# A pre-norm transformer layer on one core: the feed-forward part spread over two batches' steps, GpSimd's order and the PSUM banks changed

## What is computed

```python
x = x + attn(layernorm(x), W_qkv, W_out)      # 32 query heads, 16 key/value heads of 64, causal, ALiBi
P = einsum('bsd,dr->bsr', layernorm(x), U1)   # 256 -> 64
H = gelu(einsum('bsr,rf->bsf', P, V1) + b1)   # 64 -> 1024
Q = einsum('bsf,fr->bsr', H, U2)              # 1024 -> 64
x = x + einsum('bsr,rd->bsd', Q, V2) + b2     # 64 -> 256
```

## Time and profile before

| | us |
|---|---|
| device time, median of 3 runs | 2876.21 (2874.03 to 2881.04) |
| the profiled execution's own time | 2881.05 |
| its span, first to last instruction | 2879.3 |
| PE busy | 2680.9 (93%) |
| ACT busy | 2184.7 (76%) |
| POOL busy | 2011.7 (70%) |
| DVE busy | 1992.4 (69%) |

### The profile page before, as it was taken

The page is one execution under the profiler, slowest core; times in us unless marked ns, Lnnn a source line. Parts: engine busy times, 40 slices in busy tenths (PEclk is TensorE's granted clock), DMA queues, the critical chain, the costliest instruction groups (busy, mean ns, idle before and its releaser), DMA issues.

```text
span 2879.3 us, 83610 instructions
## 1 busy us (share of the span) xinstructions
PE 2680.9 (93%) x31112; PEld 1834.4 (64%) x31112; DVE 1992.4 (69%) x6731; ACT 2184.7 (76%) x3892; POOL 2011.7 (70%) x1816
## 2 busy tenths in 40 slices
PE   4999999999999999999999999999999999999986
PEld 1566666766666666666766667666666766667663
DVE  6767676776766767676776776767677676767753
ACT  3777878778787777878778787777878778787782
POOL 1667777777777767777677777777777677777783
PEclk8999999999999999999999999999999999999996
DMA  6444443444434344343544434344343444435420
GB/s 170 96 100 88 94 90 79 104 91 91 89 87 99 82 97 88 87 97 78 105 90 93 89 84 101 85 94 87 88 99 81 98 91 91 92 77 105 87 61 20
DMA packets 495146, 260.82 MB, mean 91 GB/s; under 512 B 317962, under 2 KB 493066, under 8 KB 494474
## 3 DMA queue, kind: packets, MB, share of 16 engines
q1 hardware_dynamic: 494740, 255.47, 40.8%
...
## 4 chain that ended last, share of the span: by engine, by line
PE 71%; ACT 8%; DVE 7%; issue 7%; POOL 5%; DMA 1%; SPq 0%; DVEq 0%; ACTq 0%; POOLq 0%
PE proj L450 31%; PE scores L450 17%; PE o_acc L450 13%; PE max_scores L450 4%; PE ffn_acc L450 4%; ACT h_f L830 2%; POOL p_lo L1090 2%; DVE max_scores L930 2%; ACT p_hi L700 2%; POOL o_hi_lo L1098 2%; ACT p_f L741 2%; ACT L741 1%; DVE h_hi L1022 1%; DMA o_t<-in_L_attn_W_out 1%; POOL h_lo L1118 1%
## 5 line engine op out<-in xcount | busy, mean ns | idle before, releaser
L1090 POOL TENSOR_TENSOR p_lo<-p_f,p_hi 128x512 f16<-128x512 f32 x1280 | 1474.4, 1159 | 564.6 <-ACT p_hi L700 564.4
L741 ACT ACTIVATE p_f<-scores 128x512 f32<-128x512 f32 x1280 | 755.6, 590 | 130.0 <-PE scores L450 126.2
L700 ACT ACTIVATE p_hi<-p_f 128x512 f16<-128x512 f32 x1280 | 800.4, 625 | 14.8
L930 DVE CUSTOM_DVE_ANT_0 max_scores<-max_scores,causal 128x384 f32<-128x384 f32 (+3 forms) x1184 | 563.3, 507 | 268.7 <-PE max_scores L450 257.7
L450 PE MATMUL scores<-q_hi_lo,k_lo_hi 128*128 128x512 f16 (+3 forms) x2048 | 614.2, 300 | 0.2 <-ACT p_f L741 0.2
L450 PE MATMUL scores<-q_hi_aug,k_hi_aug 128*128 128x512 f16 (+3 forms) x2048 | 586.5, 299 | 0.0
L450 PE MATMUL o_acc<-v_hi_one,p_lo 128*128 128x65 f16 x5120 | 518.9, 195 | 42.9 <-POOL p_lo L1090 39.9
L450 PEld LDWEIGHTS o_acc<-v_hi_one,p_lo 128*128 128x128 f16 x5120 | 471.1, 98 | 90.7 <-POOL p_lo L1090 63.2
L450 PE MATMUL o_acc<-v_hi_one,p_hi 128*128 128x65 f16 x5120 | 518.3, 194 | 0.0
L450 PE MATMUL o_acc<-v_lo,p_hi 128*128 128x64 f16 x5120 | 517.9, 193 | 0.0
L450 PEld LDWEIGHTS o_acc<-v_lo,p_hi 128*128 128x128 f16 x5120 | 468.7, 99 | 37.8
...
## 6 DMA issues: line engine op xcount, KB each, us to landing
q_hi_aug<-q_pair_hi SPq DMA_DIRECT2D x512, 64.0 KB, 2.0
q_hi_lo<-q_pair_hi SPq DMA_DIRECT2D x512, 64.0 KB, 2.0
q_hi_lo<-q_pair_lo SPq DMA_DIRECT2D x512, 64.0 KB, 2.0
k_hi_aug<-k_pair_hi SPq DMA_DIRECT2D x256, 64.0 KB, 2.0
k_lo_hi<-k_pair_hi SPq DMA_DIRECT2D x256, 64.0 KB, 2.0
k_lo_hi<-k_pair_lo SPq DMA_DIRECT2D x256, 64.0 KB, 2.0
...
```

The lines of the kernel that those rows point to most:

```text
L700: return nc.scalar.activation(out_ap, in_ap, ACT.Copy, scale=scale)
L741: nc.scalar.activation(p_f[:, k % 3, :], score_bank[k % 2][:, :], ACT.Exp).then_inc(exp_done, 1)
L930: last = nc.vector.tensor_tensor_reduce(out=bank, in0=bank, in1=causal[:, (T - 1 - qt) * P:S], scale=1.0, scalar=-3e38, op0=ALU.add, op1=A ...
L1090: nc.gpsimd.tensor_tensor(p_lo[:, slot, n, :], p_f[:, k % 3, :], p_hi[:, slot, n, :], ALU.subtract).then_inc(lo_p, 1)
```

## The change

**The feed-forward part is spread.** `FFN_PAIRS` becomes `H_PAIRS` at (13, 1), (15, 1) and, in the next body, (1, 1) and (3, 1), placed ahead of the row maxima in TensorE's segment; the casts and GpSimd's subtractions go one segment later (`SPLIT_PAIRS`); the second products go to (14, 3), (0, 3), (2, 3), (4, 3), the last step to (5, 0) and (5, 3) and the store to the end of step 5. A short body in mode TAIL, steps 0 to 5, is added at the end for the last batch.

**The second products are summed in SBUF.** Each pair has a `proj` bank of its own, and VectorE copies the first into `q_sum` and adds the other three. `ffn_acc` is gone as such; the row maxima have two banks throughout.

**GpSimd's order.** The fifth `p_lo` comes before `o_lo` in segment 0. The power for the first layer norm moves from the end of step 7 to (8, 2), the four of the second from (8 + t, 4) to (9 + t, 0). **VectorE's order and the banks**: transposing the row maxima moves from segment 1 to 2, the second layer norm one segment later.

```diff
-MAX_SEG, K_SEG, V_SEG, O_SEG = 1, 0, 4, 4
+MAX_SEG, K_SEG, V_SEG, O_SEG = 2, 0, 4, 4
-VE1_AT, NMR1_AT = (7, 4), (8, 2)
+VE1_AT, RS1_AT, NMR1_AT = (7, 4), (8, 2), (8, 4)
-RSTD2_AT = {(8 + t, 4): t for t in range(T)}
-LN2_AT = {(9 + t, 1): t for t in range(T)}
-LN2_T_AT = {(9 + t, 2): t for t in range(T)}
+RSTD2_AT = {(9 + t, 0): t for t in range(T)}
+LN2_AT = {(9 + t, 2): t for t in range(T)}
+LN2_T_AT = {(9 + t, 3): t for t in range(T)}
-FFN_PAIRS = {(13, 1): 0, (13, 3): 1, (14, 0): 2, (14, 2): 3}
-U2_PAIRS = {(13, 4): 0, (14, 0): 1, (14, 2): 2, (14, 4): 3}
-QF_AT, Y_AT = (15, 1), (15, 4)
+H_PAIRS = {(13, 1): 0, (15, 1): 1, (1, 1): 2, (3, 1): 3}
+SPLIT_PAIRS = {(13, 2): 0, (15, 2): 1, (1, 2): 2, (3, 2): 3}
+U2_PAIRS = {(14, 3): 0, (0, 3): 1, (2, 3): 2, (4, 3): 3}
+QF_AT, Y_AT, STORE_AT = (5, 0), (5, 3), 5
 def q_lag(s):
-    return 0 if s >= 13 else 1
+    return 1
         def max_place(s, n):
-            k, total = SEG * s + n, SEG * KV
-            back = next(j for j in range(1, total) if in_ffn_bank((k - j) % total) == in_ffn_bank(k))
-            return (ffn_bank if in_ffn_bank(k) else max_bank), back
+            return max_bank[(SEG * s + n) % 2], 2
             body(Count(B), LAST)
+            body(Count(B + 1), TAIL)
+        def ffn_batch(i, s):
+            return i - 1 if s >= 8 else i - 2
...
+                    if s == STORE_AT and ffn_in(i, s):
+                        done = ffn_batch(i, s)
+                        sp.wait_ge(y_done, at(2 * (done + 1) + FREE))
+                        sp.dma_start(out[done.value()].rearrange("(t p) d -> p t d", p=P), x2[:, :, :]).then_inc(y_out, 16)
...
+                def ffn_u2(f, pair):
+                    bank = next_proj(("u", pair), u_acc, f * 4 + pair + 1)
                     for c in (2 * pair, 2 * pair + 1):
+                        pe.wait_ge(hi_h, at(f * FC + c + 1))
+                        mm(bank[:, :], u2s[:, c, :], h_hi[:, c % 2, :], c % 2 == 0, False)
+                        pe.wait_ge(lo_h, at(f * FC + c + 1 + FREE))
+                        mm(bank[:, :], u2s[:, c, :], h_lo[:, c % 2, :], False, c % 2 == 1).then_inc(pe_u2, 1)
...
                         if in_stage(mode, s, ATT):
                             scores(s, n)
+                        if (s, n) in H_PAIRS and ffn_in(i, s):
+                            ffn_h(ffn_batch(i, s), H_PAIRS[s, n])
...
+                        if (s, n) in U2_PAIRS and ffn_in(i, s):
+                            f, pair = ffn_batch(i, s), U2_PAIRS[s, n]
+                            dve.wait_ge(pe_u2, at(f * FC + 2 * pair + 2))
+                            if pair == 0:
+                                dve.wait_ge(lo_qf, at(f + FREE))
+                                nc.vector.tensor_copy(q_sum[:, :], proj("u", 0)[:, :]).then_inc(u_acc, 1)
+                            else:
+                                dve.wait_ge(u_acc, at(f * 4 + pair))
+                                nc.vector.tensor_tensor(q_sum[:, :], proj("u", pair)[:, :], q_sum[:, :],
+                                                        ALU.add).then_inc(u_acc, 1)
...
                     for n in range(SEG):
+                        if n > 0 and in_stage(mode, s, ATT):
+                            low_p(SEG * (i * KV + s - ATT) + n - 1, s % 2, n - 1, SEG * s + n - 1)
+                        if n == 0 and in_stage(mode, s, ATT + 1):
+                            low_p(SEG * (i * KV + s - ATT) - 1, (s - 1) % 2, SEG - 1, (SEG * s - 1) % (SEG * KV))
                         if n == 0 and in_stage(mode, s, ATT + 2):
                             slot = (s - ATT - 2) % 2
-                        if n > 0 and in_stage(mode, s, ATT):
-                            low_p(SEG * (i * KV + s - ATT) + n - 1, s % 2, n - 1, SEG * s + n - 1)
-                        if n == 0 and in_stage(mode, s, ATT + 1):
-                            low_p(SEG * (i * KV + s - ATT) - 1, (s - 1) % 2, SEG - 1, (SEG * s - 1) % (SEG * KV))
```

More of the change, by code:

```diff
@@ L90, in before @@
     return divmod(SEG * s + n - lag, SEG)
-def in_ffn_bank(k):
-    return k % 2 == 1 and k < U2_START
 def q_segment(s):
@@ L148, with steps @@
 PROJ = {use: k % BANKS for k, use in enumerate(projection_order())}
-FFN_USES = ("ln2", "p", "h", "y")
-def last_uses(b):
-    mine = [use for use in projection_order() if PROJ[use] == b]
-    steady = [use for use in mine if use[0] not in FFN_USES]
-    return {mine[-1], steady[-1]}
 MULTIPLES = (1, 2, 4, 8, 16, 32, 64, 80, 128, 192)
 FREE = 1
-FIRST, MID, LAST = "first", "mid", "last"
+FIRST, MID, LAST, TAIL = "first", "mid", "last", "tail"
+def steps(mode):
+    return range(STORE_AT + 1) if mode == TAIL else range(KV)
 class Count:
@@ L277, in layer @@
         h_f = sb("h_f32", [P, 2, S], F32)
+        q_sum = sb("ffn_q_sum", [P, S], F32)
         x2n = h_f[:, 0, 0:D]
@@ L378, in body @@
             def body(i, mode):
-                for s in range(KV):
+                for s in steps(mode):
                     g = i * KV + s
@@ L422, in body @@
                                                o_hl[:, slot, :, :].rearrange("p a q -> p (a q)")).then_inc(ot_in[slot], 16)
-                    if s in range(OUT_LAG - 2, OUT_LAG + 2) and mode != LAST:
+                    if s in range(OUT_LAG - 2, OUT_LAG + 2) and mode in (FIRST, MID):
                         t = s - (OUT_LAG - 2)
@@ L583, in project_v @@
                     t, half = s % 8, s // 8
-                    bank = next_proj(("v", s))
+                    bank = next_proj(("v", s), lo_v, i * 8 + half * 4 + t + 1)
                     col = QD + KD + half * 512
@@ L592, in project_out @@
                     group, t = out_use(s)
-                    bank = next_proj(("out", s))
+                    bank = next_proj(("out", s), acc_done, 16 * i + s - OUT_LAG + 1)
                     if t == 0:
@@ L604, in transpose_x2 @@
                     u = (i - 1) * 4 + t
-                    bank = next_proj(("ln2", t))
+                    bank = next_proj(("ln2", t), lo_ln2, u + 1)
                     pe.wait_ge(x2n_done, at(u + 1))
@@ L612, in ffn_p @@
                     u = (i - 1) * 4 + t
-                    bank = next_proj(("p", t))
+                    bank = next_proj(("p", t), lo_pp, u + 1)
                     pe.wait_ge(lo_ln2, at(u + 1))
@@ L772, in body @@
                     for n in range(SEG):
-                        if n == q_segment(s) + 1 and mode != LAST:
+                        if n == q_segment(s) + 1 and mode in (FIRST, MID):
                             high_q(s)
@@ L832, in body @@
                             if (s, n) == QF_AT:
-                                act.wait_ge(pe_u2, at(i * FC))
-                                copy(qf_hi, ffn_bank[:, :], 1.0 / FFN_SCALE).then_inc(hi_qf, 1)
-                        if n == V_SEG and s % 8 < 4 and mode != LAST:
+                                act.wait_ge(u_acc, at((f + 1) * 4))
+                                copy(qf_hi, q_sum[:, :], 1.0 / FFN_SCALE).then_inc(hi_qf, 1)
+                        if n == V_SEG and s % 8 < 4 and mode in (FIRST, MID):
                             t, half = s % 8, s // 8
@@ L971, in body @@
                         sv, segment = before(s, n, v_lag(s))
-                        if segment == V_SEG and sv % 8 < 4 and mode != LAST:
+                        if segment == V_SEG and sv % 8 < 4 and mode in (FIRST, MID):
                             t, half = sv % 8, sv // 8
```

163 lines of the change are left out of this document (70 added, 93 removed).

## The result

The changed kernel takes **2848.26 us** (median of 4 runs, 2843.53 to 2852.71) against 2877.7 for the kernel before (4 runs, 2874.03 to 2881.04): ratio 0.9897, 95% interval 0.9885 to 0.991. It is faster, by 29 us where 80 were forecast. 2796 is missed by 52 us; 2848 lies just inside the range, at its upper end.

What follows compares the result with a forecast made beforehand. TensorE was taken to bound the kernel almost everywhere, ScalarE in step 14. Fifteen batches at -5.6 us (-84), -6 for the first body and +10 for the drain gave -80: 2796 us, range 2750 to 2850.

Steps and rivals of the forecast that it cites:

- (a): The exp behind a Gelu pair comes 0.6 us late in steps 13, 1 and 3, not 15: +1.8 a batch.
- the drain: The program's end after the middle bodies: -4 from GpSimd's order, +7 in steps 1 and 3, +6.5 last feed-forward: +10 us.
- (c): Step 7: `o_lo` behind the fifth `p_lo` delays SP's transposition 1.6 us, k 1.05 late before step 8; +1.1 with (d).
- 3.5 us a batch of new waits: All added waits of a middle batch: 1.8, 0.3, 1.1 and 0.3 us; own range 2 to 5.5.
- rival A: ScalarE bounds the steps with a pair: 2859 us, or 2828 if half of that; chance 0.2.
- What is removed: Waits for row maxima, Gelu's bank, `p_lo`, v's low part and an output block go: -9.1 us a batch.
- (b): `p_lo` behind the pair: 0.3 us late at `attend` of step 14, nothing after steps 15, 1 and 3.
- (d): Step 6's transposed maxima 3 us later, their DMAs behind the store: 0.2 to 0.8 before step 7, not lost again in (c).
- (e): VectorE's copy and three additions into `q_sum`, about 0.7 us each, four a batch: covered, taken as 0.
- The new order's saving in the drain: The fifth `p_lo` before `o_lo` on GpSimd saves about 0.7 us in each of six drain steps: -4.
- the 4.7 us of products: TensorE work missing from the first middle body, which has no earlier pairs or last product; it goes to the drain.
- B: Queue behind `o_lo`: k late in all eight odd steps, 2964 us at worst, 2880 with half of them; chance 0.08.

## Why the prediction fell short

Two steps failed, (a) for the pair in step 15 and the drain; (c) had its size too small. The prediction took 3.5 us a batch of new waits, 2 to 5.5 at the ends of its own range, 2774 to 2826 us; 6.5 were measured. The wider range holds 2848 only because it was drawn over most of rival A; that is luck.

**What is removed: right.** All waits of the earlier trace rows went, and by their spacing they were 9.9, not 9.1.

**(a) Right in three steps, wrong in the fourth.** Steps 13, 1 and 3: 0.6 forecast, 0.46 to 0.49 measured. "In step 15 ... nothing is late" is the step that failed. It asked only whether the exp of segment 4 is late, and stopped at the step's end. The instructions behind the pair in step 15 are also x's high parts, and their end is needed at (0, 1): 1.65 us a body, 25 us in all. Without table loads it is 0, and with the pair elsewhere too; the bank is 0.4 of it.

**(b) Right:** 0.3 and 0.2.

**(c) and (d): the mechanism right, the size short.** 1.1 was forecast, 1.62 measured at (7, 0) and (8, 0), and some 0.5 more at (14, 0), (3, 0) and (15, 0), where 0.3 was allowed; with it the output projections, 0.48, which wait for the same queue's transpositions and were not in the sum. Where nothing was lost at (7, 0), the transposition moved by 2.1 us, not 1.6: the fifth `p_hi` came 1.3 us after the step's start, where I had taken 0.75 from the earlier trace rows. The likely reason, which no run tests by itself, is that the steps begin sooner when TensorE no longer waits, and ScalarE's exps do not. (d) was right that what is lost before step 7 is not lost in (c) again: with the delay of the maxima taken away, (8, 0) grew by as much. With k's delay taken away (7, 0) stayed, so they are two causes.

**(e) Right:** no wait for the sum in SBUF.

Not in the sum were the 0.15 at four places where q takes k's bank, 0.6 a body: the two uses of a pair's first product now stand between k's and q's, so that q is the third use behind k. They are no part of the burst. The new order's saving in the drain held: forecast 4 over six steps, measured 3.3 with that part alone, and 1.8 behind them.

**The drain: +10 forecast, +17.4 measured.** Its steps 0 to 5 were to take 3 more and took 11.3. Three terms are missing. First, the burst was costed in its own step only, and steps 0, 2 and 4, one behind a pair, are 3.5, 1.7 and 1.3 us longer than before: where no projection covers it, `p_lo` comes late in the next step (1.8 and 1.7 us in steps 0 and 2). Second, the 4.7 us of products moved here were taken out of the first body and put nowhere, since TensorE was idle here. With GpSimd's new order alone, TensorE is busy 38.0 of the 40.9 us of these six steps, so they count; by how much is argued, not tested by itself. Third, the clock in steps 3 and 4. Behind step 5 the sum came out, 6.5 forecast and 6.1 measured, but by two errors: from the first product of the last feed-forward part to the last second product it took 22.3 us where 20 were forecast, and the attention steps ahead of it were 2.4 us faster, where the prediction had counted the new order's saving in six steps alone.

**The rivals.** A has the nearest number, 2859 or 2828 around 2848, and ScalarE's burst is the largest single cause; but its sign, an engine nearly full, is not there: 9.74 of 10.97 us in step 13. B was right in kind: alone on the kernel before, the new order makes the kernel slower by 15 us, of which the fill is 5. In the changed kernel the waits at (2, 0), (4, 0) and (6, 0) are not there; that products and projections ahead of the need hide them is argued.

**What stays open:** why the maxima's DMAs land late in some batches and not in others, in the kernel before too; what MAX_SEG costs by itself; and the spread of the fill.
